# Second router: logits as 16 extra columns of the output product, scatters behind all additions, two output banks, five groups

## The reference

```python
x = x + _L0_attn_ref(_layernorm(x), ...)   # causal softmax attention, 16 heads
x = x + _L0_ffn_ref(_layernorm(x), ...)    # 8 experts, the best 2 of each token
x = x + _L1_attn_ref(_layernorm(x), ...)   # linear attention, no softmax
x = x + _L1_ffn_ref(_layernorm(x), ...)    # 8 experts, the best 1 of each token

# third layer, per sequence:
energy = einsum('bnd,bne->bde', K, V)
out = (Q @ energy) * sqrt(3 / 64) @ wo
# fourth layer's router:
logits = x_flat @ w_gate + b_gate
route_p, route_idx = max(softmax(logits)), argmax(softmax(logits))
```

## Time and profile before

| | |
|---|---|
| median of three runs | 759.5 us |
| the profiled execution | 757.02 us, span 755.2 us |
| bridge: first matmul to the barrier's release | 520.2 to 655.8 us |
| second expert stage | 655.8 us to the end |
| mean granted clock of TensorE, whole span | 0.834 of 2.4 GHz |
| busy in the whole span: PE, DVE, ACT, POOL | 557.0, 446.6, 356.5, 336.0 us |

### The profile page before, as it was taken

One profiled execution on the slowest core, in us unless ns is written; L12 is line 12 of the kernel. 1 busy time (PEld: TensorE's weight loads), 2 busy tenths in 40 slices (PEclk: granted clock), 3 DMA queues, 4 the chain that ended last, 5 costly groups with the idle time before them and its releaser, 6 DMA issues. The chain is left out here.

```text
span 755.2 us, 15979 instructions
## 1 busy us (share of the span) xinstructions
PE 557.0 (74%) x5008; PEld 464.6 (62%) x5023; DVE 446.6 (59%) x1254; ACT 356.5 (47%) x889; POOL 336.0 (44%) x459
## 2 busy tenths in 40 slices
PE   2188999999999886540399999990564964099994
PEld 1146666666676664330399999990564853088994
DVE  5366779779879974264345555531865353646662
ACT  1015556456555654220176666661544445056662
POOL 1104453344773566567145555552414062325564
PEclk9559999999999998655599999995666555589997
DMA  6634544454544430072122222213901020433230
GB/s 150 133 84 95 105 101 99 92 116 94 122 124 96 99 90 24 21 287 85 48 62 66 67 66 67 69 47 107 355 13 36 21 86 28 128 84 99 83 101 14
DMA packets 59512, 69.22 MB, mean 92 GB/s; under 512 B 9241, under 2 KB 50657, under 8 KB 57148
## 3 DMA queue, kind: packets, MB, share of 16 engines
q1 hardware_dynamic: 50592, 52.22, 27.8%
q0 software_dynamic: 7168, 14.77, 5.8%
q10 hardware_dynamic: 1692, 1.48, 1.0%
HBM read 45.31 MB, written 23.67 MB: 91 GB/s over the span
## 5 line engine op out<-in xcount | busy, mean ns | idle before, releaser
L644 DVE TENSOR_REDUCE mx<-max_ps 128x2 f32<-128x512 f32 (+1 forms) x192 | 128.3, 687 | 53.3 <-PE max_ps L305 51.2
L1369 DVE COPY wb<-wpack 128x1156 f32 x112 | 85.3, 802 | 83.9 <-issue 81.2
L1418 ACT ACTIVATE hT<-h_ps,wb 128x128 f32<-128x128 f32 x448 | 121.9, 386 | 27.1 <-PE h_ps L1450 27.1
L485 ACT ACTIVATE pT<-sc_ps 128x1536 f32<-128x1536 f32 x64 | 92.8, 1451 | 76.9 <-PE sc_ps L333 76.6
L1450 PE MATMUL h_ps<-xT,wb 128*128 128x128 f32 x896 | 113.4, 281 | 0.9 <-ACT xT L1408 0.9
L1315 POOL DMA_INDIRECT expert_rows<-yt,go x72 | 75.8, 1053 | 75.7 <-DVE go L1361 64.4
L1450 PEld LDWEIGHTS h_ps<-xT,wb 128*128 128x128 f32 x896 | 107.7, 197 | 2.0 <-ACT xT L1408 1.7
L1461 PE MATMUL y_ps<-wb,hT 128*128 128x128 f32 x896 | 108.9, 275 | 0.0
L1461 PEld LDWEIGHTS y_ps<-wb,hT 128*128 128x128 f32 x896 | 104.4, 192 | 0.0
L305 PE MATMUL max_ps<-kst,qst 72*128 72x256 bf16 (+1 forms) x512 | 77.0, 256 | 4.8 <-DMA qst<-parts_scratch 4.1
L880 POOL TENSOR_TENSOR turn<-eps 128x1 f32<-128x1 f32 x64 | 12.4, 194 | 144.8 <-ACT pT L485 144.8
(11 more groups left out here) (245 smaller groups left out, 963.2 us busy)
## 6 DMA issues: line engine op xcount, KB each, us to landing
kst<-parts_scratch SPq DMA_DIRECT2D x48, 192.0 KB
qst<-parts_scratch SPq DMA_DIRECT2D x135, 64.0 KB
wpack<-in_wpack SPq DMA_DIRECT2D x2, 4112.0 KB, 15.1
parts_scratch<-parts SPq DMA_DIRECT2D x16, 384.0 KB, 3.5
xt<-expert_queues SPq DMA_DIRECT2D x40, 129.0 KB, 2.1
xt<-expert_queues SPq DMA_DIRECT2D x72, 64.5 KB
back<-expert_rows SPq DMA_DIRECT2D x16, 256.0 KB, 5.0
expert_queues<-rxr,rseats POOLq DMA_INDIRECT x96
```

The source lines that it names most:

```text
L485: nc.scalar.activation(pT[u][:], sc_ps[:].rearrange("p a s -> p (a s)"), ACT.Exp, scale=float(DH) ** -0.5).then_inc(probs_ready, 1)
L644: nc.vector.reduce_max(mx[:, s, h0:h0 + n], max_ps[:, (k + 1) % 2, :].rearrange("p (h k) -> p h k", h=n), axis=AX.X).then_inc(unit_reduced, 1)
L1369: nc.vector.tensor_copy(wb[r][:, s, :], wpack[:, bass.ds(es[s], 1), :].rearrange("p a f -> p (a f)")).then_inc(w_ready, 1)
L1418: last = nc.scalar.activation(hT[par][:, s, c, :], h_ps[par][:, s, c * RT:(c + 1) * RT], ACT.Relu, bias=wb[r][:, s, FF + c:FF + c + 1])
```

## The change

The router's logits are linear in the sum of two things: the output of the linear attention, and `x` itself, which is the normalised sequence times its deviation (less its mean). So both can be had from the product that forms the output. The matrix `m` gets 16 more columns: eight that give the output's share of the logits (`B` is widened by `B` times the centred router weights, so that `second_product` makes them), and eight constant ones, the centred router weights, that give the share of the normalised sequence. `outputs` becomes 144 columns wide for each tile. VectorE copies the 16 columns into `terms` in `add_x`, and for a group forms the logits (`join_terms`: times the old deviation, plus; then in `choose` times the new inverse deviation, plus the bias). `turn_rows`, `take_rows`, `logits` and `take_logits` go. At the bridge's start three small products and six small copies prepare the constants.

GpSimd does all 32 additions first and then all 32 scatters; ScalarE weighs nine sequences before the loop, where it was seven. `outputs` alternates between two PSUM banks. There are five groups (8, 8, 8, 4, 4 tiles), a choice is made one round after the group's statistics, its rank in the next round and its seat in the one after. The results of the first expert stage are fetched in pieces of 2, 2, 4, 4, 4, 4, 4 and 8 tiles, where each was 4.

```diff
-LATER = ((0, 8), (8, 8), (16, 4), (20, 4), (24, 4), (28, 4))
+LATER = ((0, 8), (8, 8), (16, 8), (24, 4), (28, 4))
+PIECES = ((0, 2), (2, 2), (4, 4), (8, 4), (12, 4), (16, 4), (20, 4), (24, 8))
...
-    NCH, AHEAD = 8, 6
+    AHEAD, WEIGHED, LAG, LAST = 6, 9, 3, 4
+    W = D + E
...
-        x_ps, g_ps, t1_ps, m_ps, o_ps, xr_ps, lg_ps, rank_ps = (ps(n) for n in ("x_ps", "g_ps", "t1_ps", "m_ps", "o_ps", "xr_ps", "lg_ps", "rank_ps"))
+        x_ps, g_ps, t1_ps, m_ps, rank_ps = (ps(n) for n in ("x_ps", "g_ps", "t1_ps", "m_ps", "rank_ps"))
+        o_ps = [ps(f"o_ps{i}") for i in range(2)]
...
-            return [g for g, (first, n) in enumerate(LATER) if (first + n) // TPS + 1 + n // 4 == i]
+            return [g for g, (first, n) in enumerate(LATER) if (first + n) // TPS + 1 == i]
...
-            for c in range(AHEAD):
-                add(c)
-            sent = 0
-            for i in range(SLOTS):
-                if i + AHEAD < NSEQ:
-                    add(i + AHEAD)
-                while sent < NT and sent < 2 * (i - 7) and i + AHEAD < NSEQ:
-                    scatter(sent)
-                    sent += 1
-            for j in range(sent, NT):
+            for j in range(NT):
+                pool.wait_ge(weighed, j + 1)
+                nc.gpsimd.tensor_tensor(x[:, j, :], back[:, 0, j, :], x[:, j, :], ALU.add).then_inc(added, 1)
+            for j in range(NT):
                 scatter(j)
...
-                nc.scalar.copy(m_sb[i % 2][:], m_ps[:, 0:D]).then_inc(m_ready, 1)
+                nc.scalar.copy(m_sb[i % 2][:, 0:W], m_ps[:, 0:W]).then_inc(m_ready, 1)
...
-            def take_rows(h):
-                g, first, n = halves[h]
-                act.wait_ge(xrT_done, h + 1)
-                if h >= 2:
-                    act.wait_ge(lg_done, h - 1)
-                nc.scalar.copy(xrT[h % 2][:, 0:n * P], xr_ps[:, 0:n * P]).then_inc(xrT_ready, 1)
...
+            nc.scalar.mul(B[:, 0:D], m_ps[:, 0:D], (3.0 / DL) ** 0.5)
+            nc.scalar.mul(BT[:], x_ps[:, 0:D], (3.0 / DL) ** 0.5)
+            for i in range(2):
+                nc.scalar.copy(m_sb[i][:, W:W + E], g_ps[:, 0:E])
+            nc.scalar.copy(wrc[:], g_ps[:, 0:E]).then_inc(ab_ready, 1)
+            act.wait_ge(ab_done, 2)
+            nc.scalar.copy(B[:, D:W], rank_ps[:, 0:E]).then_inc(ab_ready, 1)
...
-            for c in range(2, AHEAD + 1):
+            for c in range(2, WEIGHED):
                 weigh(c)
-            deviations(1, 4, 8)
+                if c == AHEAD:
+                    deviations(1, 4, 8)
...
-                nc.tensor.matmul(m_ps[:, 0:D], t1[i % 2][:], B[:], start=True, stop=True).then_inc(m_done, 1)
+                nc.tensor.matmul(m_ps[:, 0:W], t1[i % 2][:], B[:], start=True, stop=True).then_inc(m_done, 1)
...
-                if i:
-                    pe.wait_ge(x_added, i)
+                if i >= 2:
+                    pe.wait_ge(x_added, i - 1)
                 for s in range(TPS):
-                    last = nc.tensor.matmul(o_ps[:, s * P:(s + 1) * P], xnT[i % 2][:, s * P:(s + 1) * P], m_sb[i % 2][:], start=True, stop=True)
+                    last = nc.tensor.matmul(o_ps[i % 2][:, s * (W + E):(s + 1) * (W + E)], xnT[i % 2][:, s * P:(s + 1) * P], m_sb[i % 2][:], start=True, stop=True)
...
-            def turn_rows(h):
-                g, first, n = halves[h]
-                pe.wait_ge(xr_ready, first + n)
-                if h:
-                    pe.wait_ge(xrT_ready, h)
-                for k in range(n):
-                    last = nc.tensor.transpose(xr_ps[:, k * P:(k + 1) * P], rxr[:, first + k, 0, 0:D], ident[:])
-                last.then_inc(xrT_done, 1)
-
-            def logits(h):
-                g, first, n = halves[h]
-                pe.wait_ge(xrT_ready, h + 1)
-                if h:
-                    pe.wait_ge(lg_read, h)
-                for k in range(n):
-                    last = nc.tensor.matmul(lg_ps[:, k * E:(k + 1) * E], xrT[h % 2][:, k * P:(k + 1) * P], t["wr1"][:], start=True, stop=True)
-                last.then_inc(lg_done, 1)
...
             def add_x(i):
+                out = o_ps[i % 2][:, 0:TPS * (W + E)].rearrange("p (s d) -> p s d", s=TPS)
                 dve.wait_ge(o_done, i + 1)
...
+                nc.vector.tensor_tensor(rxr[:, i * TPS:(i + 1) * TPS, 1, 0:D], out[:, :, 0:D], x[:, i * TPS:(i + 1) * TPS, :], ALU.add)
+                nc.vector.tensor_copy(terms[:, i * TPS:(i + 1) * TPS, :], out[:, :, D:W + E]).then_inc(x_added, 1)
...
+            def join_terms(first, n):
+                ts = slice(first, first + n)
+                link(nc.vector.tensor_tensor(lg[:, ts, :], terms[:, ts, E:2 * E], over_e(ntmp[:, 4, ts]), ALU.mult))
+                nc.vector.tensor_tensor(lg[:, ts, :], lg[:, ts, :], terms[:, ts, 0:E], ALU.add)
...
+                link(nc.vector.tensor_tensor(src, src, over_e(rstd[:, ts]), ALU.mult))
+                link(nc.vector.tensor_tensor(src, src, t["br1"][:].unsqueeze(1).to_broadcast([P, n, E]), ALU.add))
...
-                for g in choices(i - 1):
+                for g in choices(i - (LAG - 1)):
                     seat(g)
+                    gate(g)
+                if 0 <= i - 1 < NSEQ:
+                    last = add_x(i - 1)
+                    if i in routed:
+                        link(last)
+                        dve.wait_ge(xn_ready, i)
+                        join_terms(*LATER[routed[i]])
+                        scales(*LATER[routed[i]])
```

More of the change, by code:

```diff
@@ L1557, in _ @@
             wait_results(sp, t, 2, 0)
-            for c in range(NCH):
+            for c, (first, n) in enumerate(PIECES):
                 for k in range(2):
-                    sp.dma_start(back[:, k, c * CT:(c + 1) * CT, :], ys_v[k, c]).then_inc(loaded[c], 16)
+                    sp.dma_start(back[:, k, first:first + n, :], ys_v[k][:, first:first + n, :]).then_inc(loaded[c], 16)
             load_pack(nc, sp, t, dram, 1)
@@ L1749, in _ @@
                     outputs(i - 1)
-                for h in rows_at(i):
-                    turn_rows(h)
+                for g in choices(i - 1):
+                    rank(g)
         @block.vector
@@ L1886, in _ @@
                     inverse(roots(i - 1), *LATER[routed[i - 1]])
-                    shifts(routed[i - 1])
-                if i in closes:
-                    n, k = SCALED[closes[i]]
-                    scales(TPS * n, TPS * k)
-                if 0 <= i - 1 < NSEQ:
-                    last = add_x(i - 1)
-                    if i in routed:
-                        link(last)
-                        dve.wait_ge(xn_ready, i)
-                        scales(*LATER[routed[i]])
-                for g in choices(i - 1):
-                    gate(g)
                 for g in choices(i):
```

83 lines of the change are left out of this document (33 added, 50 removed).

## The result

The changed kernel takes **719.9 us** (median of four runs, 717.09 to 720.5) against 759.3 us for the kernel before on the same chip (four runs, 757.74 to 762.06). The ratio is 0.947, 95% interval 0.9432 to 0.9508. The rival "VectorE alone sets the pace" gave 720.7 us.

A forecast was written before the change was run, and what follows sets the result against it. It took hand-offs in the logits chain, ending in GpSimd's scatters and drain, as the bound. 542.3 + 48.8 + 7.8 + 21.0 + 4.9 opened the barrier at 624.8, 31.0 us earlier: 728.5 us, range 720 to 740.

The forecast's parts named there:

- VectorE alone sets the pace: Rival: TensorE's clock stays up in the bridge, the 7.8 us of waits vanish, gain 38.8, time 720.7 us; chance 0.15.
- Start of the loop: Bridge start: four more weighings on ScalarE take 1.28 us, moving VectorE's first addition from 541.04 to 542.3 us.
- VectorE to the third gate: VectorE's own work in the bridge, from its first addition to the third group's gate: 48.8 us.
- Waits of VectorE: VectorE's waits for TensorE's outputs before the third gate: six rounds (2, 3, 10 to 13) at 1.3 us, 7.8 us.
- The second bank: Claim that a second output bank lets outputs go ahead of VectorE, removing the other eight waits; no separate size.
- GpSimd: From the third gate, 16 scatters without a gap, later gates in time: 21.0 us, to 619.9.
- the stall of the tenth round: Old bridge: VectorE waits 3.15 us for GpSimd's last two additions, TensorE idles 7.2 us; forecast to go.
- Drain: GpSimd's drain after its last scatter at the bridge's end: 4.9 us, bounds 2.6 and 4.9.
- The second expert stage: The stage after the bridge's barrier: length taken as unchanged, with 2 us either way.
- Sum: The barrier at the bridge's end opens at 624.8 instead of 655.8 us, 31.0 us earlier.
- The rival of a wait in every round: Rival: TensorE's outputs come late in all 14 rounds, 1.3 us each; gain 20.6, time 738.9 us; chance 0.18.

The follow-up runs named there:

- f3: Changed kernel with VectorE's copy of the logit terms done three times, two into spare buffers: 722.3 us, ratio 0.95.
- f0: The changed kernel run again unedited, on a chip of the first kind: 720.8 us, ratio 0.9461.
- f1: Changed kernel with one output bank and the old turned rows and router product done again, result unused: 738.1 us, ratio 0.97.
- f2: Changed kernel with TensorE's transposes and Gram products of each round done three times: 725.8 us, ratio 0.9544.
- a2: Changed kernel with one output bank instead of two: 719.9 us, ratio 0.9466.
- a3: Changed kernel with GpSimd's old order of additions and scatters put back: 719.1 us, ratio 0.9462.
- a1: Kernel before the change with one edit, GpSimd doing all 32 additions ahead of the scatters: 756.1 us, ratio 0.9952.

## Why the prediction was right in kind and too small

*Start of the loop*: right. Forecast 542.3, measured 542.24.

*VectorE to the third gate*: right but for 1.1 us. From 542.24 to 591.62 are 49.4 us, less 1.7 of waits 47.7; forecast 48.8. The new copy, bounded by 0 and 0.42 and taken as 0.13, has a length of 0.18 and by f3 costs 0.10.

*Waits of VectorE*: **this step failed.** "Now VectorE waits for the outputs 11.7 us in all in the bridge, nine times, 1.3 us each. So 6 x 1.3 = 7.8 us." It was 1.7 (3.0 in f0), which is 6.1 us of the miss. Of the six rounds that I named only the second, the eleventh and the twelfth had a wait, of 0.25, 0.16 and 1.26 us. The price was too high already by the old rows: the nine waits include the one ahead of the first addition and two behind the third gate, and the six between sum to 5.6 us, 0.9 each. And it came from a loop in which TensorE also turned the rows. f1 shows what these did: with them put back and their result unused, the waits up to the third gate are 14.5 us where they are 3.0 without. TensorE's round of 3.56 us is another matter: it is from the first rounds, where no turned rows stand, and it came back there (542.00 - 538.33 = 3.67). Between the second round and the third gate the granted clock was 1.00 but for two short stretches: 0.57 from 560 to 564 us, and 0.78 and 0.64 in the two rounds from 575.5 to 581.4, those with the two later waits; TensorE's round there was 581.38 - 578.44 = 2.94. Without the turned rows TensorE waits for VectorE instead, and the granted clock is 0.87 (f0: 0.80) in the stretch where it was 0.60. The rule of the Trainium skill (TensorE: Matmul & The Clock Gate, What's actually happening), that the throttled state is the default and activity releases it, I had read as speaking for a denser list. f2 agrees with it: with more work on TensorE its granted clock was 1.00 up to the third gate, where it was 0.84 without. But in f1, also with more work, it was 0.75 there, so more work alone does not tell which way the clock goes. Between the kernels before and after the rows show a granted clock that rose while TensorE's busy share fell, from 63.4 of 99.2 us to 34.8 of 60.7; how much of either comes from the other they do not tell. That the rival which the rule favoured came within 1 us of the time (720.7 against 719.9) does not show the rule; it is in part luck, since the waits of 1.7 us that it leaves out are made up by a shorter list and a shorter drain.

"The second bank ... is what makes the other eight waits vanish": wrong. With one bank they are gone too (a2).

*GpSimd*: right. Forecast 21.0 us from the gate to the last scatter's issue, measured 612.4 - 591.6 = 20.8, with no gap; the later gates came in time, and the additions ahead of the scatters held nothing back. That the order itself would be worth something in the new kernel, as the stall of the tenth round suggested, is refuted by a3.

*Drain*: a size was off. I chose 4.9 between bounds of 2.6 and 4.9 by the row that was nearest; it is 2.9, another 2.0 us.

*The second expert stage* took 100.0 us against 99.4, within the 2 us allowed.

*Sum*: 31.0 forecast + 6.1 waits + 1.1 list + 0.2 scatters + 2.0 drain = 40.4; measured 40.5. That is the end of the bridge; the second stage was 0.6 us longer, and by the medians the gain is 39.4 us, so the miss in the time is 8.6. All four errors pointed the same way. The bounds of the terms held them, but not the range: taken together these bounds (7.8 for the waits, 2.3 for the drain, 2 for the rest) reach to 716, and I let the range stop at 720, the rival's time. The rival "VectorE alone sets the pace" comes closest; f3 bears it out to two thirds, and f2 shows that TensorE is not altogether out of it. The rival of a wait in every round is out: up to the third gate ScalarE's rows stand ahead of rounds 7, 8, 11 and 12, and of these only the eleventh and the twelfth had a wait. Ahead of the twelfth's ScalarE had finished the rows and stood idle for TensorE:

```profile
579.97 0.37 ACT L1598 COPY xnT<-x_ps 128x256 f32<-128x256 f32 x1 [0.43 <-PE g_ps L1669]
```

By parts, where runs tell it: about 17 of the 40 us come back when the turned rows are put back into the lists of TensorE and ScalarE ahead of the outputs, with their work, their waits for each other and the lower clock that went with them (f1). GpSimd's order is worth 3.5 us in the old kernel (a1) and none in the new one; bank and number of groups none. The rest, about 20 us, was not taken apart by a run. The waits of VectorE for the turned rows' logits (17.7 us before, none after) are of that size, but the new places of choice, rank, seat and gate in the rounds came with the same change, and so did the end of the waits for the exponential and the root (13.9 us before, 0.5 after); no run has the one without the other.

## What to carry to other kernels

When a stage is bound by hand-offs, add up the waits of the engine that the others return to, here VectorE, and hold the sum against the length of the stage: here 42 us fewer waits and 3 us more work made the stretch 38.5 us shorter. A step removed from an in-order engine helps twice: its own chain goes, and all that stood behind it in the list comes earlier; so waits for other results may not be carried over from the old loop at their old price. An overlap read from a record's length is too dear for small VectorE operations; take start to start.

## What the runs showed of the hardware

- Independent small copies of 32 columns out of PSUM follow each other every 0.10 us on VectorE, although each record is 0.18 us long (f3).
- Indirect scatters of 128 rows are issued by GpSimd every 1.27 us, also with the other engines busy; in f1 the last three intervals were 1.4 to 1.5 us. The drain behind the last took 2.8 to 5.7 us in these kernels.
- More work on TensorE went with a higher granted clock in f2 (1.00, busy 45.8 of 53.6 us up to the third gate, against 0.84 and 36.0 of 50.6 in the changed kernel) and with a lower one in f1 (0.75, busy 48.7 of 62.5 us), where it brought waits for ScalarE with it. So the price of added matmuls can't be read from their number alone.
- The gain depends on the chip: ratio 0.946 to 0.947 where the kernel before takes 759 us, and 0.9575 where it takes 788.
